# Layer-norm statistics of two sequences by one interleaved BATCH_NORM_STATS2, without aggregates

## The reference

```
k  = layernorm(x)                       # over the 256 channels, eps 1e-5, no weights
x1 = x + wkv(time_decay, time_first, k, ctx)
     # per channel, over t: aa, bb decay by exp(-exp(time_decay)),
     # y_t = (e^(u+k_t) v_t + aa) / (e^(u+k_t) + bb), then aa += e^k_t v_t, bb += e^k_t
n  = layernorm(x1)
g, u = (n @ gate_w.T) * gate_s, (n @ up_w.T) * up_s       # 256 -> 704
out = x1 + ((silu(g) * u) @ down_w.T) * down_s            # 704 -> 256
```

## Time and profile before

| what | value |
|---|---|
| median of three runs | 104.21 us |
| span of the profiled execution, from its first to its last instruction | 102.7 us |
| PE busy | 91.5 us (89%) |
| DVE busy | 80.0 us (78%) |
| ACT busy | 78.2 us (76%) |
| POOL busy | 66.8 us (65%) |
| granted TensorE clock | full speed throughout |
| BATCH_NORM_STATS2 | 32 instructions |
| BATCH_NORM_AGGREGATE | 32 instructions |

### The profile page before, as it was taken

One profiled execution on the slowest core, in us unless ns is written; L12 is line 12 of the kernel. 1 busy time (PEld: TensorE's weight loads), 2 busy tenths in 40 slices (PEclk: granted clock), 3 DMA queues, 4 the chain that ended last, 5 costly groups with the idle time before them and its releaser, 6 DMA issues.

```text
span 102.7 us, 1698 instructions
## 1 busy us (share of the span) xinstructions
PE 91.5 (89%) x504; PEld 75.1 (73%) x504; DVE 80.0 (78%) x169; ACT 78.2 (76%) x136; POOL 66.8 (65%) x96
## 2 busy tenths in 40 slices
PE   3958976998799999996999999999999999999930
PEld 3957965996596778875788887887888778888610
DVE  1789899969998999799999998999863806543450
ACT  4371999989997879999999999999959634655300
POOL 2016465998799999894399779827899701764500
PEclk9999999999999999999999999999999999999999
DMA  1999999999000000000005000000500000400005
GB/s 32 307 379 405 403 321 388 343 387 343 34 0 0 0 0 10 0 0 0 0 0 203 1 6 0 0 3 0 203 1 0 0 6 3 183 21 0 0 28 189
DMA packets 6475, 10.78 MB, mean 105 GB/s; under 512 B 576, under 2 KB 3648, under 8 KB 6336
## 3 DMA queue, kind: packets, MB, share of 16 engines
q1 hardware_dynamic: 6320, 10.62, 28.9%
q10 hardware_dynamic: 144, 0.03, 0.2%
HBM read 8.55 MB, written 2.10 MB: 104 GB/s over the span
## 4 chain that ended last, share of the span: by engine, by line
PE 27%; POOL 17%; ACT 15%; issue 14%; DMA 11%; DVE 6%; SPq 4%; POOLq 2%; DVEq 1%; ACTq 0%
PE ps_f L728 16%; DMA xc<-x_ch 11%; POOL hl L346 11%; PE ps_d L745 4%; ACT ek L405 4%; PE ps_f L756 3%; ACT L374 2%; POOL xc L311 2%; ACT nt L434 2%; SPq L228 2%; PE ps_x L698 2%; ACT xh L445 2%; DVE h L631 1%; POOL rs L323 1%; POOLq L59 1%
## 5 line engine op out<-in xcount | busy, mean ns | idle before, releaser
L728 PE MATMUL ps_f<-xh,wgu_r 128*128 128x512 f32 (+1 forms) x94 | 36.3, 391 | 0.6 <-DVE xl L616 0.4
L728 PE MATMUL ps_f<-xl,wgu_r 128*128 128x512 f32 (+1 forms) x94 | 35.1, 378 | 0.0
L346 POOL TENSOR_TENSOR hl<-h,hh 128x512 fp32r<-128x512 f32 x20 | 25.6, 1293 | 9.3 <-ACT hh L476 9.2
L631 DVE SCALAR_TENSOR_TENSOR h<-ps_f,vec,sil 128x512 f32<-128x512 f32 x20 | 14.9, 744 | 9.2 <-PE ps_f L728 6.2
L728 PEld LDWEIGHTS ps_f<-xh,wgu_r 128*128 128x128 f32 x94 | 17.7, 188 | 5.5 <-issue 1.4
L728 PEld LDWEIGHTS ps_f<-xl,wgu_r 128*128 128x128 f32 x94 | 17.7, 188 | 2.8
L756 PE MATMUL ps_f<-ident 128*128 128x128 f32 x110 | 15.5, 296 | 1.9 <-POOL ident L266 1.6
L465 ACT ACTIVATE sil<-ps_f,vec 128x512 f32<-128x512 f32 x20 | 13.7, 688 | 4.0 <-PE ps_f L728 3.8
L745 PE MATMUL ps_d<-hh,wd_r 128*128 128x512 f32 x40 | 16.3, 407 | 0.1
L756 PEld LDWEIGHTS ps_f<-ident 128*128 128x128 f32 x110 | 14.5, 211 | 2.1 <-POOL ident L266 1.6
L476 ACT ACTIVATE hh<-h 128x512 fp32r<-128x512 f32 x20 | 12.5, 629 | 4.6 <-DVE h L631 4.5
(11 more groups left out here) (73 smaller groups left out, 133.8 us busy)
## 6 DMA issues: line engine op xcount, KB each, us to landing
xt<-x_tok SPq DMA_DIRECT2D x8, 256.0 KB, 7.3
xc<-x_ch SPq DMA_DIRECT2D x4, 512.0 KB, 9.6
out_ch<-xc SPq DMA_DIRECT2D x8, 256.0 KB, 2.5
wgu<-w_gu SPq DMA_DIRECT2D x1, 1408.0 KB, 8.6
vc<-v_ch SPq DMA_DIRECT2D x2, 512.0 KB, 9.4
wd<-w_d SPq DMA_DIRECT2D x1, 768.0 KB, 10.0
vt<-v_tok SPq DMA_DIRECT2D x2, 256.0 KB, 5.3
vt<-v_tok SPq DMA_DIRECT2D x1, 512.0 KB, 12.3
```

Source lines behind the costliest of these rows:

```text
L346: nc.gpsimd.tensor_tensor(hl[:, m, :], h[:, n % HS, :], hh[:, m, :].bitcast(F32), ALU.subtract).then_inc(s_hl, 1)
L631: nc.vector.scalar_tensor_tensor(h[:, n % HS, :] if m < FULL else up, up, vec[r, V_US + m:V_US + m + 1], sil[r, n % 2, :], ALU.mult, ALU.m ...
L728: last = nc.tensor.matmul(ps_f[:, i % RING, ts], w, a, start=c == 0 and x is xh, stop=c == CC - 1 and x is xl)
```

## The change

The two sequences of a unit are given to one `bn_stats` as one row of 512 elements, read alternately: channel 0 of the first sequence, channel 0 of the second, channel 1 of the first, and so on. The instruction's even half is then the first sequence and its odd half the second, and its six outputs are count, mean and sum of squared deviations of each. No aggregate is needed. The sum of squared deviations is turned into the variance by a factor 1/C where ACT and POOL add eps. Those who waited for `s_mv1` and `s_mv2` wait for `s_st1` and `s_st2`. The lists of the engines keep their order, less the aggregates.

```
-        st1 = sb("st1", [P, B, 6])
-        mv1 = sb("mv1", [P, B, 2])
+        st1 = sb("st1", [P, B, 3])
...
 def bias1(u):
-                nc.gpsimd.tensor_tensor(mr1[:, q], mv1[:, q, 0], rs1[:, q], ALU.mult).then_inc(s_mr1, 1)
+                nc.gpsimd.tensor_tensor(mr1[:, q], st1[:, q, 1], rs1[:, q], ALU.mult).then_inc(s_mr1, 1)
...
 def rstd2(u):
-                    pool.wait_ge(s_mv2, u + 1)
-                    nc.gpsimd.tensor_scalar(ve2[:, seqs(u)], mv2[:, seqs(u), 1], 1.0, EPS, ALU.mult, ALU.add).then_inc(s_ve2, 1)
+                    pool.wait_ge(s_st2, u + 1)
+                    nc.gpsimd.tensor_scalar(ve2[:, seqs(u)], st2[:, seqs(u), 2], 1.0 / C, EPS, ALU.mult, ALU.add).then_inc(s_ve2, 1)
...
 def rstd1(u):
-                act.wait_ge(s_mv1, u + 1)
+                act.wait_ge(s_st1, u + 1)
-                nc.scalar.activation(lv1[:, q], mv1[:, q, 1], ACT.Ln, bias=epsc[:, 0:1]).then_inc(s_lv1, 1)
+                nc.scalar.activation(lv1[:, q], st1[:, q, 2], ACT.Ln, scale=1.0 / C, bias=epsc[:, 0:1]).then_inc(s_lv1, 1)
...
             def stats1(u):
                 dve.wait_ge(s_xt[u], 16)
-                for b in range(u * UB, (u + 1) * UB):
-                    last = nc.vector.bn_stats(st1[:, b, :], xt[:, b, :])
-                last.then_inc(s_st1, 1)
-
-            def aggr1(u):
-                dve.wait_ge(s_st1, u + 1)
-                for b in range(u * UB, (u + 1) * UB):
-                    last = nc.vector.bn_aggr(mv1[:, b, :], st1[:, b, :])
-                last.then_inc(s_mv1, 1)
+                nc.vector.bn_stats(st1[:, seqs(u), :].rearrange("p b k -> p (b k)"),
+                                   xt[:, seqs(u), :].rearrange("p b c -> p c b")).then_inc(s_st1, 1)
...
             def stats2(u):
                 dve.wait_ge(s_x1T, u + 1)
-                for b in range(UB):
-                    last = nc.vector.bn_stats(st2[:, u * UB + b, :], x1_bank(u)[:, b * C:(b + 1) * C])
-                last.then_inc(s_st2, 1)
...
+                nc.vector.bn_stats(st2[:, seqs(u), :].rearrange("p b k -> p (b k)"),
+                                   x1_bank(u).rearrange("p (b c) -> p c b", b=UB)).then_inc(s_st2, 1)
...
-            lift_(); stats1(0); aggr1(0); stats1(1); stats1(2); decay_(); aggr1(1); aggr1(2); stats1(3); scan_e(0)
-            aggr1(3); denom(0); scan_p(0); scan_e(1); numer(0); denom(1); scan_p(1); scan_e(2); numer(1); denom(2)
+            lift_(); stats1(0); stats1(1); stats1(2); decay_(); stats1(3); scan_e(0)
+            denom(0); scan_p(0); scan_e(1); numer(0); denom(1); scan_p(1); scan_e(2); numer(1); denom(2)
...
```

More of the change, by code:

```diff
@@ L108, in build @@
         yk = sb("yk", [P, 2, SEG, T])
-        st2 = sb("st2", [P, B, 6])
-        mv2 = sb("mv2", [P, B, 2])
+        st2 = sb("st2", [P, B, 3])
         ve2 = sb("ve2", [P, B])
@@ L143, in build @@
         s_wsum, s_wcnt, s_flag = (sem(n) for n in ("s_wsum", "s_wcnt", "s_flag"))
-        s_st1, s_mv1, s_lv1, s_rs1, s_ve1, s_rs1p, s_mr1, s_nb1, s_ek = (sem(n) for n in (
-            "s_st1", "s_mv1", "s_lv1", "s_rs1", "s_ve1", "s_rs1p", "s_mr1", "s_nb1", "s_ek"))
+        s_st1, s_lv1, s_rs1, s_ve1, s_rs1p, s_mr1, s_nb1, s_ek = (sem(n) for n in (
+            "s_st1", "s_lv1", "s_rs1", "s_ve1", "s_rs1p", "s_mr1", "s_nb1", "s_ek"))
         s_pk, s_eT, s_pT, s_mp, s_se, s_sp = (sem(n) for n in ("s_pk", "s_eT", "s_pT", "s_mp", "s_se", "s_sp"))
@@ L150, in build @@
             "s_den", "s_num", "s_ln", "s_rd", "s_y", "s_v0", "s_x1"))
-        s_x1T, s_st2, s_mv2, s_ve2, s_rs2a, s_rs2, s_mr2, s_nb2, s_nt, s_nT, s_xh, s_xl = (sem(n) for n in (
-            "s_x1T", "s_st2", "s_mv2", "s_ve2", "s_rs2a", "s_rs2", "s_mr2", "s_nb2", "s_nt", "s_nT", "s_xh", "s_xl"))
+        s_x1T, s_st2, s_ve2, s_rs2a, s_rs2, s_mr2, s_nb2, s_nt, s_nT, s_xh, s_xl = (sem(n) for n in (
+            "s_x1T", "s_st2", "s_ve2", "s_rs2a", "s_rs2", "s_mr2", "s_nb2", "s_nt", "s_nT", "s_xh", "s_xl"))
         s_gate, s_up, s_sil, s_h, s_hh, s_hhp, s_hl, s_hx, s_dn, s_fin, s_set, s_res = (sem(n) for n in (
@@ L273, in bias1 @@
                     i = RSTD_POOL.index(u) + 1
-                    pool.wait_ge(s_mv1, u + 1)
-                    nc.gpsimd.tensor_scalar(lv1[:, q], mv1[:, q, 1], 1.0, EPS, ALU.mult, ALU.add).then_inc(s_ve1, 1)
+                    pool.wait_ge(s_st1, u + 1)
+                    nc.gpsimd.tensor_scalar(lv1[:, q], st1[:, q, 2], 1.0 / C, EPS, ALU.mult, ALU.add).then_inc(s_ve1, 1)
                     pool.wait_ge(s_ve1, i)
@@ L324, in rstd2 @@
                     pool.wait_ge(s_rs2, u - GU + 1)
[L325 removed]
+                nc.gpsimd.tensor_tensor(mr2[:, seqs(u)], st2[:, seqs(u), 1], rs2[:, seqs(u)], ALU.mult).then_inc(s_mr2, 1)
                 pool.wait_ge(s_mr2, u + 1)
@@ L421, in rstd2a @@
             def rstd2a(u):
-                act.wait_ge(s_mv2, u + 1)
-                nc.scalar.activation(ve2[:, seqs(u)], mv2[:, seqs(u), 1], ACT.Ln, bias=epsc[:, 0:1]).then_inc(s_ve2, 1)
+                act.wait_ge(s_st2, u + 1)
+                nc.scalar.activation(ve2[:, seqs(u)], st2[:, seqs(u), 2], ACT.Ln, scale=1.0 / C, bias=epsc[:, 0:1]).then_inc(s_ve2, 1)
                 act.wait_ge(s_ve2, u + 1)
@@ L656, in finish_c @@
                 residual(GROUPS - 1, c)
-            lift_(); stats1(0); aggr1(0); stats1(1); stats1(2); decay_(); aggr1(1); aggr1(2); stats1(3); scan_e(0)
-            aggr1(3); denom(0); scan_p(0); scan_e(1); numer(0); denom(1); scan_p(1); scan_e(2); numer(1); denom(2)
-            stats1(4); stats1(5); stats2(0); aggr1(4); aggr1(5); aggr2(0); stats2(1); publish(); aggr2(1); scan_e(3)
+            lift_(); stats1(0); stats1(1); stats1(2); decay_(); stats1(3); scan_e(0)
+            denom(0); scan_p(0); scan_e(1); numer(0); denom(1); scan_p(1); scan_e(2); numer(1); denom(2)
+            stats1(4); stats1(5); stats2(0); stats2(1); publish(); scan_e(3)
             scan_p(2); denom(3); numer(2); stats1(6); low_n(0); scan_p(3); low_n(1); numer(3); stats2(2); mulp(4)
[L662 to L667, removed]
+            gated(0); gated(1); scan_p(4); scan_e(4); gated(2); stats1(7); gated(3); low_n(2); numer(4)
+            denom(4); stats2(3); gated(4); gated(5); mulp(5); scan_e(5); scan_p(5)
+            denom(5); low_n(3); numer(5); stats2(4); low_rest(5); scan_e(6); gated(6); mulp(6); gated(7)
+            finish(0); low_n(4); denom(6); stats2(5); gated(8); gated(9); scan_p(6); numer(6); scan_e(7)
+            low_n(5); gated(10); gated(11); mulp(7); stats2(6); denom(7); low_rest(11); gated(12); scan_p(7)
+            numer(7); gated(13); finish(1); low_n(6); gated(14); stats2(7); gated(15); gated(16); gated(17)
             low_n(7); low_rest(17); gated(18); gated(19); finish(2); gated(20); gated(21); gated(22); gated(23)
```

## The result

The kernel after took 105.05 us (median of 13 runs, 104.42 to 105.6), the kernel before 104.19 (13 runs in turn with it): ratio 1.0081, interval 1.0057 to 1.0106. The forecast was 103.9. In a second batch the ratio was 1.0043 [1.0011, 1.0074]. The loss is small and real, and the forecast had the wrong sign. Some executions of every kernel are disturbed and some 1.5 to 3 us longer, and all ratios leave them out.

The account below looks back on a forecast made before the run. PE was taken as the bound, full from 48 to 82 us, so DVE savings gain only before 48 us. Sum -0.3 us: span 102.7 to 102.4, plus 1.5 outside, 103.9 us; own range 103.6 to 104.1, all cases 103.5 to 105.8.

Parts of the forecast that it names:

- Step 4: stats1(7) ahead of gated(3): shorter by 0.06 us; with 0.25 from up(1), gate(5) at 38.30 comes 0.3 us earlier.
- a PE stream as dense as before: PE from e_T(6), near 47.0 us, onward: products as dense as in the kernel before.
- Rival A: Strided reads at half rate: 1.20 us per statistics instruction, total +1.4 us, 105.6 us; chance 0.30.
- Aggregates and DVE's total: Dropping aggregates saves 3.6 us busy; DVE held 3.5 us less in all, busy 80.0 to about 74, or 75.
- So whatever DVE saved earlier, 21.86 stays: stats2(1) on DVE waits for PE's x1_T(1), so its start at 21.86 us is fixed.
- step 1: ACT no longer waits 0.27 us for aggr2(1) at 22.94; silu(0) at 30.88 comes 0.25 us earlier.
- rival C: Nothing moves: gate(0), not ACT, holds silu(0), and POOL's chain sets x1_T(4); 104.15 us, chance 0.13.
- Steps 2 and 3: Shorter stats1(6): low_n(0) and PE's first product at 27.97 come 0.19 us earlier; up(1) at 31.71 follows silu(0), 0.25 earlier.
- Step 5: Aggregates and statistics before gated(4), which waits for PE: their 0.5 us becomes more waiting, nothing more.
- Rival B: gated(4) follows DVE's queue, PE's hole before e_T(6) closes: 0.5 us on top of 0.3, 103.4 us; chance 0.12.
- Step 6: gated(4) to e_T(6) shift by 0.3 us; x1_T(4) behind needs POOL's add_y(4) at 47.57, so it just fits.
- After 47.28 PE has work without a hole: PE from e_T(6) at 47.28 us to the last products: no idle holes.

Follow-up runs that it names:

- before_mem5: Kernel before with five one-column memsets at the start of DVE's stream: 104.18 us, ratio 0.9997.
- before_moved: Kernel before with st1, mv1, st2, mv2 allocated last and gaps instead, putting the tiles PE reads at the changed kernel's addresses: 104.67 us, 1.0049.
- nops17: Changed kernel with 17 no-operations in DVE's list, none of which appear in the trace: 105.26 us, 1.009.
- padmem17: Changed kernel padded back to the old addresses, with 17 memsets at the start of DVE's stream: 104.05 us, 0.9972.
- padmem1: Changed kernel padded back to the old addresses, with one memset at the start of DVE's stream: 103.8 us, 0.9982.
- x128mem1: Changed kernel with one memset and 128 bytes of gap behind st2: 103.93 us, 0.9993.
- x64mem1: Changed kernel with one memset and 64 bytes of gap behind st2: 103.67 us, 0.9965.
- best_again: Repeat of x64mem1 (changed kernel, one memset, 64 bytes of gap): 103.93 us, 0.9971.
- after_again: Changed kernel, unedited, run again for a second trace and more times: 104.86 us, 1.0043 against the kernel before.
- same_addresses: Changed kernel with unused pads behind st1 and st2, so later tiles lie at their old addresses; no memset: 104.33 us, 1.0024.

## Why the prediction was wrong, step by step

Two steps failed. Step 4's sum took every instruction to start as its wait ends; gated(1)'s started 0.45 us behind its wait, and gate(3) and what follows it came 0.4 us later. And "from there a PE stream as dense as before", on which the prediction rested its last 50 us, put at nothing what measured 0.48 us.

**The duration was right.** 0.69 forecast; 0.700 and 0.693 us measured, in SBUF and PSUM. Rival A, strided reads at half rate, falls. The Trainium skill's "Advanced Engine Details and Errata", "Memory Cachelines", asks for a penalty where each access opens another line; this case's trace does not agree for DVE and this operation: 1,024 bytes between neighbours, and an element costs what the elementwise rows cost. **Aggregates and DVE's total**: 76.5 us. The 3.5 us that DVE was to be held less are exactly the 3.5 by which its busy time fell; "near 75", from the busy times of single records, was 1.5 too low, because neighbouring records overlap.

**"So whatever DVE saved earlier, 21.86 stays" failed**, though not by DVE. stats2(1) came at 21.06 in the trace after: the x1(0) transposes stand anywhere between 16.9 and 18.05 us in the 17 traces, as xc lands. What up(1) does then fits all traces of the old kernel as the later of two: 13.66 us after the transposes (13.66, 13.66, 13.67, 13.67 measured), or 18.31 us after ACT's reciprocal of unit 0 (before_mem5; before_moved, where both come together, has 18.35). In the changed kernel the second is the same, 18.31 or 18.32 in eleven traces; the first is 13.32, seen alone in one trace (nops17). So **step 1's** 0.25 us exist, as 0.34, where the landing is late, and not where ACT's own list, which has no hole from there on, is the longer. Put into both formulas, the 17 traces' own times give a gain of 0 in eleven and of 0.04 to 0.34 in six, 0.08 us on the mean (an estimate; 13.32 rests on one trace). The kernel as given, with an early landing, was on ACT's list (30.46 for the earlier trace rows's 30.88):

```profile
22.43 0.20 ACT L396 ACTIVATE rs<-lv 128x4 f32<-128x4 f32 x1
22.54 0.28 ACT L422 ACTIVATE ve<-st,epsc 128x2 f32<-128x2 f32 x1
...
30.46 1.26 ACT L463 ACTIVATE sil<-ps_f,vec 128x512 f32<-128x512 f32 x2
```

ACT's wait of 0.27 us is gone here, but the old kernel with an early landing (before_moved) had none either; in its other three traces it is 0.04, 0 and 0.13 us:

```profile
22.12 0.20 ACT L400 ACTIVATE rs<-lv 128x4 f32<-128x4 f32 x1
22.25 0.29 ACT L426 ACTIVATE ve<-mv,epsc 128x2 f32<-128x2 f32 x1
```

I had read the row at 22.94 as the kernel's and it was that execution's. This is half of rival C: nothing comes of a faster DVE where ACT itself is the chain. The 0.41 us that up(1) gained in the profiled pair are the landing's and not the change's: by the fit, the old kernel with this trace's times would also have come at 31.30 (reciprocal at 12.99, and 18.31).

**Steps 2 and 3** held as mechanisms: PE's first product at 27.73 still waits 0.49 us for low_n(0), and up(1) follows ACT.

**Step 4**, the 0.06 us of stats1(7), is found, at least in its size: up(1) to e_T(6) is 15.49 to 15.53 us in padmem17, padmem1, x128mem1, x64mem1 and best_again against 15.54 to 15.57 in the old kernel's four traces at the same distances, 0 and 64.

**"0.25 + 0.06 = 0.3 us earlier" for gate(5), which is step 4's sum, failed in the kernel as it was given.** gated(1) stands between up(1) and gate(3); I had taken a wait's end to be the start of what follows it. It stood 0.45 us behind its wait instead of 0.05 in after, after_again, nops17 and same_addresses (15.92 to 15.98 us from up(1) to e_T(6)), and not in the seven kernels that have a memset more (15.49 to 15.57), whatever their addresses. This took back the 0.41 that up(1) had gained.

**Step 5** held, as stated: idle time before gated(4), with the same start.

```profile
36.77 0.71 DVE L530 BATCH_NORM_STATS2 st<-xt 128x6 f32<-128x512 f32 x1
37.38 0.74 DVE L615 SCALAR_TENSOR_TENSOR h<-ps_f,vec,sil 128x512 f32<-128x512 f32 x1
...
41.85 0.75 DVE L615 SCALAR_TENSOR_TENSOR h<-ps_f,vec,sil 128x512 f32<-128x512 f32 x1 [0.96 <-issue]
```

0.96 us of idle time where the earlier trace rows have 0.47: the 0.5 us of step 5. **Rival B** falls: gated(4) follows PE, and the hole ahead of e_T(6) is 0.84 us for 0.85.

**Step 6** could not be seen in the kernel as given, since nothing moved. In the kernels without the delay e_T(6) moved with up(1). x1_T(4), 0.60 us behind it in the old kernel, still stood at 0.60 in four traces and at 0.64 to 0.66 in padmem17, padmem1, x64mem1 and best_again, where it had to wait for POOL's add_y(4): "just fits" was close to its limit.

**"After 47.28 PE has work without a hole" and "a PE stream as dense as before" is the step that, with the late instruction, decided the sign.** There was no hole, and the stream was still slower. The prediction counted instructions and waits and had no term for the distance between products. From e_T(6) to the end it cost 51.30 - 50.82 = 0.48 us. The stretches show how such a thing hides: PE is at 34.00 of 34.00 us from 48 to 82 in both, with one record fewer after, and DVE's saving lies there as idle time.

```profile
31.30:48.00 16.70, 15.45 (x73) 11.50 (x74) 14.72 (x23) 14.43 (x27) 15.14 (x22) 1.00 0.01 2
48.00:82.00 34.00, 34.00 (x166) 27.68 (x166) 28.04 (x43) 30.87 (x47) 25.15 (x33) 1.00 0.09 31
```

The account in ratios: the change proper -0.1 to -0.3 us (the three kernels above), the late instruction +0.3 to +0.5 (same_addresses, 1.0024, less each of these three, from different batches), the addresses +0.5 (before_moved, 1.0049): together +0.8 (same_addresses and before_moved added), for +0.86 in the first batch and +0.45 in the second. The forecast's -0.3 had the right sign for the change itself and is the largest of the three values; the steps that gave it, 1 and 4, come to 0.1 us by the traces' own account (0.08 and some 0.04). What it had no term for outweighed it three times and more.

What stays open: why the spacing depends on that distance, whether the weights or a tile that lies with them is the partner, and what in the chip takes the 0.45 us of the late instruction. The transfers that follow are seen in time only; no run held them back. The one attempt to place the boundary elsewhere at a cost (before_mem5) missed.

## What to carry to other kernels

An edit that only drops instructions and shrinks tiles also moves every tile allocated behind and every later instruction's place in its engine's stream. When a saving off the critical path comes out slower, compare the distance between identical back-to-back products in both traces first, and restore the addresses with padding, one run, before looking for a mechanism in the edit. Look second for a wait that has ended and an instruction that follows it by 0.45 us rather than 0.05; one harmless instruction earlier in the list moves it. Such side effects, 0.4 and 0.5 us here, are larger than this edit's own gain.

## What was not expected of the hardware

- 512-column fp32 products started 227.3 to 233.5 ns apart on the mean (80 to 99 us), ordered by the distance of their two tiles in SBUF modulo 256 bytes (0, 64: closer together; 128, 192: further apart), at a granted clock of 1.00 in that stretch of every trace.
- An instruction of DVE, number 63 and again 191, started 0.45 and 0.42 us after its wait had ended, where 0.04 to 0.05 is usual; the second one, at 91.26 us, cost nothing: from e_T(6) to the end it is 50.78 us in same_addresses with it and 50.84 in padmem17 without.
- One BATCH_NORM_STATS2 over two interleaved rows of 256 takes 0.70 us where two take 0.76 and their aggregates 0.16 more, and neighbours 1,024 bytes apart cost no more than adjacent ones.
